# Three re-orderings in a fused attention and expert kernel: a GpSimd weighting ahead of a norm's statistics, a ScalarE eviction ahead of a split norm, and a conversion between two table loads

## The reference

```python
x = x + attention(layernorm(x), ctx, ctx)          # one head, softmax over 120 keys
h = layernorm(x)
probs = softmax(h @ router_w.T)                    # 8 experts
k = argmax(actor(h)) + 1                           # a small gelu network picks how many experts
scores = where(rank(probs) < k, probs, 0)
for e in range(8):                                 # hidden width 336
    out += scores[e] * ((silu(h @ gate_w[e].T) * (h @ up_w[e].T)) @ down_w[e].T)
x = x + out
```

## Time and profile before

| | |
|---|---|
| median of 3 runs | 774.19 us (774.03 to 774.57) |
| the profiled execution, its own time | 773.71 us |
| its span in the trace | 771.7 us |
| TensorE busy | 753.3 us |
| VectorE, GpSimd, ScalarE busy | 613.8, 574.1, 568.7 us |

### The profile page before, as it was taken

The page is one execution under the profiler, slowest core; times in us unless marked ns, Lnnn a source line. Parts: engine busy times, 40 slices in busy tenths (PEclk is TensorE's granted clock), DMA queues, the critical chain, the costliest instruction groups (busy, mean ns, idle before and its releaser), DMA issues.

```text
span 771.7 us, 13806 instructions
## 1 busy us (share of the span) xinstructions
PE 753.3 (98%) x3771; PEld 376.1 (49%) x3771; DVE 613.8 (80%) x1365; ACT 568.7 (74%) x1002; POOL 574.1 (74%) x618
## 2 busy tenths in 40 slices
PE   7988999999999999999999999999999999999997
PEld 4544444444545445454554545445454544544443
DVE  6879878887887878787797877888787787878765
ACT  5977777777777767877767777777877767777664
POOL 2577978869696886968688596886968687686763
PEclk9999999999999999999999999999999999999999
DMA  9200111202121120302112030120202101010100
GB/s 346 56 25 15 41 29 21 63 14 56 15 69 28 27 70 2 79 14 52 42 26 54 14 81 14 26 68 19 61 14 67 29 15 28 1 41 1 28 1 27
DMA packets 58429, 32.44 MB, mean 42 GB/s; under 512 B 34960, under 2 KB 53520, under 8 KB 58384
## 3 DMA queue, kind: packets, MB, share of 16 engines
q1 hardware_dynamic: 58096, 31.43, 15.9%
q10 hardware_dynamic: 288, 0.48, 0.2%
HBM read 20.07 MB, written 4.22 MB: 31 GB/s over the span
## 4 chain that ended last, share of the span: by engine, by line
PE 85%; DVE 4%; ACT 4%; issue 3%; POOL 2%; DMA 1%; SPq 0%; ACTq 0%; POOLq 0%; DVEq 0%
PE bank L536 26%; PE bank L537 25%; PE bank L538 25%; PE bank L446 2%; PE bank L424 2%; PE bank L532 1%; PE bank L435 1%; DVE bank L1379 1%; POOL weighted L1067 1%; PE bank L519 1%; DVE hid_lo L1385 1%; PE bank L491 1%; ACT L881 1%; ACT L876 1%; PE bank L510 1%
## 5 line engine op out<-in xcount | busy, mean ns | idle before, releaser
L1067 POOL TENSOR_TENSOR weighted<-silu,score_bc 128x512 f32<-128x512 f32 x336 | 428.2, 1285 | 139.2 <-ACT silu L842 134.4
L1379 DVE SCALAR_TENSOR_TENSOR bank<-bank,h_scale,weighted 128x512 f32<-128x512 f32 x336 | 253.5, 754 | 103.2 <-PE bank L538 90.7
L836 ACT ACTIVATE hid_hi<-bank 128x512 f16<-128x512 f32 x336 | 200.2, 596 | 154.3 <-DVE bank L1379 153.4
L1385 DVE TENSOR_TENSOR hid_lo<-bank,hid_hi 128x512 f16<-128x512 f32 x336 | 228.8, 681 | 30.0 <-ACT hid_hi L836 30.0
L842 ACT ACTIVATE silu<-bank,silu_scale 128x512 f32<-128x512 f32 x336 | 230.0, 684 | 23.6 <-PE bank L538 18.5
L536 PE MATMUL bank<-xn_lo,up_hi 128*128 128x512 f16 x336 | 127.4, 379 | 4.7 <-DVE hid_lo L1385 4.6
L536 PE MATMUL bank<-xn_lo,gate_hi 128*128 128x512 f16 x336 | 127.8, 380 | 0.2 <-ACT silu L842 0.2
L536 PE MATMUL bank<-hid_lo,down_hi 128*128 128x512 f16 x336 | 127.4, 379 | 0.2 <-DVE hid_lo L1385 0.2
L537 PE MATMUL bank<-xn_hi,gate_lo 128*128 128x512 f16 x336 | 127.5, 380 | 0.0
L538 PE MATMUL bank<-xn_hi,gate_hi 128*128 128x512 f16 x336 | 127.4, 379 | 0.0
L537 PE MATMUL bank<-hid_hi,down_lo 128*128 128x512 f16 x336 | 127.3, 379 | 0.0
(11 more groups left out here) (186 smaller groups left out, 790.4 us busy)
## 6 DMA issues: line engine op xcount, KB each, us to landing
x_in<-in_x SPq DMA_DIRECT2D x16, 256.0 KB, 2.9
out<-out_sb SPq DMA_DIRECT2D x16, 256.0 KB, 2.4
xt_in<-in_x_t SPq DMA_DIRECT2D x14, 256.0 KB, 2.7
row_bc<-row_kept SPq DMA_DIRECT2D x14, 256.0 KB, 3.8
ctx_in<-in_ctx_t SPq DMA_DIRECT2D x14, 240.0 KB, 2.7
raw_gate<-in_gate_t SPq DMA_DIRECT2D x3, 448.0 KB, 6.2
raw_up<-in_up_t SPq DMA_DIRECT2D x3, 448.0 KB, 7.7
raw_down<-in_down_t SPq DMA_DIRECT2D x3, 448.0 KB, 9.7
```

What stands on the lines that cost most here:

```text
L836: af(hid_hi[j % HRING][:], up_bank[j % U_BANKS][:], ACT.Copy).then_inc(hid_hi_ready, 1)
L1067: g.tensor_tensor(weighted[j % RING][:], silu[j % RING][:], score_bc[par][:], ALU.mult)\
L1379: v.scalar_tensor_tensor(up_bank[j % U_BANKS][:], up_bank[j % U_BANKS][:], h_scale[:], weighted[j % RING][:], ALU.mult, ALU.mult).then_inc ...
L1385: v.tensor_tensor(hid_lo[j % HRING][:], up_bank[j % U_BANKS][:], hid_hi[j % HRING][:], ALU.subtract)\
```

## The change

1. GpSimd, turn 0: `rstd_2(1)` moves from `j == 0` to `j == 1`, so that `weigh` of tile 2 runs ahead of it.
2. ScalarE, turn 0: `values(5, x0)` moves from `j == 3` to the head of what stands at `j == 2`. `norm2(1, 0, BB)`, four instructions at `j == 2`, becomes two instructions at `j == 2` behind it and two at `j == 3`.
3. ScalarE, every turn: `high` of tile 9 (tile 10 in turn 0) moves from the head of `j == 10 + late(t)` to the end of `j == 9 + late(t)`, between the exponentials and the load of the silu table. In turn 15, which has no exponentials, the order stays as it was.

```diff
@@ ScalarE, turn(t, par)
-                    if is_tile(TILES * t + j - 1):
+                    if is_tile(TILES * t + j - 1) and j != 10 + late(t):
                         if j >= 1:
                             high(t, j - 1)
...
                     if isinstance(t, int) and t == 0 and j == 2:
-                        norm2(1, 0, BB)
+                        values(5, x0)
+                        norm2(1, 0, 2)
                     if isinstance(t, int) and t == 0 and j == 3:
-                        values(5, x0)
+                        norm2(1, 2, BB)
...
                         if is_block(t + 2):
                             exps_by_batch(t + 2, par)
+
+                    if j == 9 + late(t) and is_tile(TILES * t + j):
+                        high(t, j)
+                    if j == 9 + late(t) and (is_block(t + 1) or is_block(t + 2)):
                         nc.scalar.preload_act_table(ACT.Silu)
@@ GpSimd, turn(t, par)
-                    if isinstance(t, int) and t == 0 and j == 0:
+                    if isinstance(t, int) and t == 0 and j == 1:
                         rstd_2(1)
```

## The result

The changed kernel takes 769.78 us (median of 5 runs, 769.68 to 769.87) against 774.13 (5 runs, 772.51 to 774.57). The ratio is 0.9947, 95% interval 0.9932 to 0.9961. Forecast were 770.3 us and a range of 768.3 to 772.6. The span of the profiled executions fell from 771.7 to 767.8 us, which is the span that was forecast.

What follows compares the result with a forecast made beforehand. TensorE, busy 753.3 of 771.7 us, was taken as the bound, with VectorE holding it next. Early stretch 2.1 plus turns 1 to 3 1.8 made 3.9 us: 774.2 - 3.9 = 770.3 us, range 768.3 to 772.6.

Steps and rivals of the forecast that it cites:

- The first edit: Turn 0, GpSimd: tile 2's multiply fills a 1.02 us hole, `weigh` 3 starts at 39.15, VectorE's 1.21 us wait closes.
- The second edit: wait gone, clock up, halves of TensorE's loss kept as new waits: Turn 0: keys' wait goes, clock stays up; half of TensorE's 4.1 us returns as shorter waits; early stretch gains 2.1.
- Then VectorE had waited 0.71 for `up` 4, which is now long done: Turn 0, VectorE: its 0.71 us wait for `up` 4 goes too, making it 1.92 us early.
- The third edit in turns 1 to 3: `low` 9 comes 1.28 us earlier; 0.59 of 0.76 us is kept per turn, 1.8 us in three turns.
- 0.76 won at first: Turns 1 to 3: `up` 12 no longer waits for `low` 9, 0.76 us before the next holder takes some back.
- The third edit in turn 0: Gives nothing: ScalarE is full, so TensorE arrives earlier and waits longer; the wait moves from `up` 13 to `gate` 16.
- The loop: Turns 4 to 13: TensorE has no wait to lose; 0 taken, bound 1.0 us lost if `silu` 12 slips.
- Contention: Early stretch: a GpSimd filled up earlier could slow two `weight_low` instructions, 0.7 us; the term was kept at 2.1.
- Early stretch larger: Rival, turn 0: VectorE is not the holder, the whole 4.1 us arrives, 768.3 us; chance 0.08.
- The loop gives back: Rival: `silu` 12 slips 0.1 in each of ten turns, 0.4 to 1.0 us lost, 770.7 to 771.3; chance 0.12.
- Waiting for `hidden` 9: Rival: `high` 9 must wait for `hidden` 9, stalling ScalarE every turn; with 0.6 us excess 776.3 us; chance 0.03.

Runs made afterwards that it cites:

- third edit alone: Kernel before with only the conversion of tile 9 (10 in turn 0) moved ahead of the silu load: 772.61 us against 774.09, ratio 0.9989.
- the wait filled: Kernel before with 11 useless matmuls in TensorE's 2.8 us wait ahead of the keys of block 6: 772.73 us against 774.16, ratio 0.9985.
- the second edit alone: Kernel before with only the eviction of block 5's values ahead of the norm, and the norm in two halves: 772.85 us, ratio 0.9989.
- the lowest group of before: Fastest cluster of the unchanged kernel's runs: 11 of 35 runs, at 772.5 to 773.1 us.
- the router-first kernel: Changed kernel with GpSimd's router work ahead of the weighting of tile 12 (13 in turn 0): 768.14 us, ratio 0.9925.
- the part taken away: Changed kernel with the eighth weights part converted by GpSimd at `j == 11` of turn 0 instead of by ScalarE: 769.48 us, ratio 0.9945.
- the first two edits alone: Kernel before with the `rstd_2(1)` move and the eviction ahead of the split norm, without the conversion move: 771.59 us, ratio 0.9974.

## Why the prediction was right, step by step

- **The first edit.** Right in place, and in size for VectorE's first hole. Tile 2 fills the hole, `weigh` 3 starts at 39.09, VectorE's 1.21 us are gone.
- **The second edit: wait gone, clock up, halves of TensorE's loss kept as new waits.** Right for the profiled execution: 1.88 of 1.92 at `hidden` 4, 2.23 of 2.13 at `hidden` 7, 0.9 of 1.1 us of wait before the actor product. Wrong in why VectorE's holes of 0.71 and 0.21 were there. The step "Then VectorE had waited 0.71 for `up` 4, which is now long done" charged them to TensorE's lateness, whatever its clock; they are the half clock's alone. With the clock up (third edit alone, or the wait filled) neither is there, and the second edit alone is then worth nothing. That the sum came out is in part luck: the execution that was read, like some two thirds of the runs, had the half clock. The step also named VectorE as the holder all the way. From 45.55 us on it is ScalarE, which runs without a gap to `up_hi`; a hole of 0.38 us that VectorE had for `up` 5, and that the sum does not have, only made VectorE's hole for `up_hi` longer (1.55 to 2.02). Against the lowest group of before, the whole change is worth 772.8 - 769.8 = 3.0 us instead of 4.3. One term was sized on one execution as if it were the kernel's.
- **The third edit in turns 1 to 3.** 0.59 each forecast, 0.57, 0.59 and 0.56 measured; and `up` 14 waits 0.25, 0.18 and 0.19, as forecast. That the router chain holds the rest was argued there and is shown by the router-first kernel. The chain has one more link than was named: `route_ahead` cannot end before the multiply that runs beside it. The "0.76 won at first" was an idle time and is 0.93 from start to start; the 0.59 was taken from starts, and so it is not touched by this.
- **The third edit in turn 0.** Nothing forecast; the wait moved to `gate` 16 with 1.13 us. Right, and ScalarE's weights part was the cause at `gate` 16, since the wait fell to 0.21 with the part taken away.
- **The loop.** 0 taken, right; mean turn length unchanged within 0.01 us (turn 4 to 5: 46.15 and 46.16). The load does wait until the conversion is out (287.97 + 0.60 = 288.57, load at 288.59), but the conversion overlaps the last exponential, and `silu` 12 moved against `gate` 14 by 0.01 us.
- **Contention.** No loss was taken in the early stretch. The first `weight_low` there took 1.34 us instead of 1.14, the second 1.13 instead of 1.15: 0.2 of the feared 0.7. The third took 1.37 instead of 1.49, so 0.1 came back. The row of 1.49 was not due to a fuller GpSimd: 0.54 us of an `xn_lo` instruction were left to run when it started. The Trainium skill (GPSIMD Engine Reference, Key points) states that GpSimd contends with VectorE instructions that have two SBUF inputs, and gives no size. The trace agrees for `weight_low` and `route_ahead`, 0.41 to 1.48 us for the same `route_ahead`, and shows that what counts is how much of the running GpSimd instruction is left, not how busy GpSimd is.
- **The rivals.** Early stretch larger: refuted by the first two edits alone. The loop gives back: refuted by the ledger of turns. Waiting for `hidden` 9: it ends at 285.08 + 0.76 = 285.84, 2.1 us before the conversion at 287.97, so it never decided; no run placed it beyond that point.

## What to carry to other kernels

When the engine that bounds the kernel waits, first ask which engine it would wait for next: here 4.1 us of TensorE's loss were worth the 2.25 that VectorE and ScalarE allowed. Then ask which part of the price was idle time and which was the clock behind it, and look at more than one execution: a wait behind which the clock may fall makes the time fall into groups, and a few useless matmuls in it tell the two apart. Count a wait of TensorE from start to start and not by its idle time. Small work that frees a later instruction on a second engine (the router work) belongs in the hole ahead of a long multiply, not behind it.

## What the runs showed of the hardware that was not expected

- After the same 2.77 us of idleness TensorE's granted clock was 0.50 in one profile (1.2 GHz) and 1.00 in another (2.4 GHz). It was 0.50 behind a wait of 1.94 us and 1.00 behind waits of 1.57 and 2.45. What decides it is not shown. The price was 1.1 us between profiles and 1.4 between medians at the keys, and 1.7 us at 230 us. By their times, about two thirds of the runs of the kernel before pay it (24 of 35).
- A VectorE instruction with two SBUF inputs that starts beside a GpSimd multiply ends 0.28 us (128x256) or 0.94 to 0.96 us (128x896) behind the end of that multiply: 0.41 to 1.48 us for one and the same instruction. The multiply that follows does not slow it, and is itself slowed, up to 2.22 us instead of 1.27.
- A transposing DMA of the token halves landed late in some executions, at 230 us: waits of 1.57 and 1.94 us in two profiles, none in the changed kernel's.
